# One block for the three stages of a deformable layer, smaller convolution rectangles, and a product moved to VectorE

## What is computed

```python
def deform_block(x, ow, ob, dw, pw, pb, K):
    offsets = conv2d(x, ow, ob, K // 2)             # 2*K*K channels: dy, dx for each tap
    out = deform_depthwise(x, offsets, dw, K, K // 2)  # bilinear samples of x at tap + offset, times dw[tap], summed over taps
    return conv2d(out, pw, pb, 0)
c3, c5, c7 = jnp.split(x, 3, axis=1)
out = jnp.concatenate([deform_block(c3, ..., 3), deform_block(c5, ..., 5), deform_block(c7, ..., 7)], axis=1)
return out * se_weight(out, fc1_w, fc2_w)           # gates from the mean and the maximum over the pixels
```

## Time and profile before

| | |
|---|---|
| median of the runs | 6606.05 us |
| the profiled execution, its own time | 6606.96 us |
| its span in the trace | 6604.7 us |
| PE busy | 88% of the span |
| VectorE busy | 73% |
| ACT busy | 59% |
| GpSimd busy | 12% |
| TensorE's granted clock, mean | 0.946 of full |

### The profile page before, as it was taken

How to read it: one execution, slowest core, us unless ns; L and a number is a source line. 1 busy time by engine, 2 the same in 40 slices (tenths; PEclk the granted TensorE clock), 3 DMA queues, 4 the chain that set the end, 5 groups by cost and what they waited for, 6 DMA issues and landing times. The chain is left out here.

```text
span 6604.7 us, 121718 instructions
## 1 busy us (share of the span) xinstructions
PE 5836.1 (88%) x45996; PEld 3998.1 (61%) x45996; DVE 4831.0 (73%) x10089; ACT 3905.2 (59%) x5362; POOL 782.4 (12%) x780
## 2 busy tenths in 40 slices
PE   5999999999977888988989989899889899699798
PEld 2554454454434556875568855588655688455598
DVE  6887887787765778887788877798777888344433
ACT  3766776676652557875567855578755787112142
POOL 2222211222202002001011000110100100000000
PEclk9999999999998999999989999999999899899898
DMA  4111111112104445545445545455544454211598
GB/s 145 43 56 55 40 44 55 49 39 59 44 23 134 105 105 123 124 110 118 105 117 118 119 97 129 99 126 121 117 105 108 114 124 111 96 46 41 145 234 199
DMA packets 198408, 651.46 MB, mean 99 GB/s; under 512 B 61753, under 2 KB 68849, under 8 KB 154915
## 3 DMA queue, kind: packets, MB, share of 16 engines
q1 hardware_dynamic: 177747, 604.65, 37.2%
q0 software_dynamic: 19968, 37.78, 2.2%
HBM read 538.56 MB, written 65.59 MB: 91 GB/s over the span
## 5 line engine op out<-in xcount | busy, mean ns | idle before, releaser
L2367 PE MATMUL b_p<-b_work,b_hkt 64*128 64x144 f32 (+37 forms) x27520 | 2116.5, 309 | 253.1 <-DVE b_acc L2238 149.7
L2367 PEld LDWEIGHTS b_p<-b_work,b_hkt 64*128 64x128 f32 x27520 | 1966.0, 195 | 479.9 <-DVE b_work L2313 283.2
L2313 DVE TENSOR_TENSOR b_work<-b_work 128x140 f32<-128x140 f32 (+26 forms) x5312 | 1605.5, 353 | 228.6 <-PE b_p L2367 174.7
L2208 ACT ACTIVATE b_work<-b_work,b_mcol 128x512 f32<-128x512 f32 (+6 forms) x1328 | 764.9, 647 | 1021.4 <-DVE b_work L2313 883.3
L530 ACT ACTIVATE a_ex<-a_p_t 128x1024 f32<-128x1024 f32 x512 | 523.9, 1023 | 427.3 <-PE a_p_t L466 424.5
L2212 ACT ACTIVATE b_work<-b_work,b_mrow 128x544 f32<-128x544 f32 (+6 forms) x1328 | 762.2, 645 | 0.0
L2238 DVE SCALAR_TENSOR_TENSOR b_acc<-b_p,b_dwc,b_acc 128x323 f32<-128x323 f32 (+14 forms) x1088 | 621.6, 574 | 184.5 <-PE b_p L2367 184.5
L596 DVE TENSOR_REDUCE a_nm<-a_p_x 128x1 f16<-128x1024 f32 x512 | 624.3, 1219 | 154.0 <-PE a_p_x L455 145.8
L1779 PE MATMUL b_p<-b_hp,b_ow 128*98 128x512 f32 x1568 | 721.4, 611 | 0.0
L602 DVE TENSOR_TENSOR a_el<-a_ex,a_eh 128x1024 f16<-128x1024 f32 x512 | 682.1, 1332 | 7.0 <-ACT a_eh L535 6.9
L535 ACT CAST a_eh<-a_ex 128x1024 f16<-128x1024 f32 x512 | 535.4, 1046 | 54.8 <-ACT a_ex L530 3.8
(11 more groups left out here) (224 smaller groups left out, 5811.6 us busy)
## 6 DMA issues: line engine op xcount, KB each, us to landing
b_work<-sampling_positions SPq DMA_DIRECT2D x666, 512.0 KB, 6.5
d_win<-merged_kernels SPq DMA_DIRECT2D x192, 263.0 KB, 6.7
b_xin<-x SPq DMA_DIRECT2D x24, 1024.0 KB, 9.8
a_xr<-in_x SPq DMA_DIRECT2D x12, 1536.0 KB, 10.2
x<-a_xr SPq DMA_DIRECT2D x9, 1536.0 KB, 6.1
b_xr<-x SPq DMA_DIRECT2D x13, 1024.0 KB, 18.2
x<-b_xr SPq DMA_DIRECT2D x13, 1024.0 KB, 4.6
a_xh<-in_x SPq DMA_DIRECT2D x8, 1536.0 KB, 8.6
```

The source lines that it names most:

```text
L2208: last = e.activation(rx[:, u, xo[c]:xo[c + 1]].rearrange("p (a b) -> p a b", a=H), pp[:, b, 1, :].rearrange("p (a b) -> p a b", a=H)[:, : ...
L2313: e.tensor_tensor(S[:, k % NS, 0:(r1 - r0) * w].rearrange("p (a b) -> p a b", b=w), rx[:, u, xo[cc]:xo[cc + 1]].rearrange("p (a b) -> p a ...
L2367: last = e.matmul(G[:, a0 - top:z0 - top, c0 - left:c1 - left], hkt[64 * s:64 * s + 64, SIDE * cr + cc, :], S[64 * s:64 * s + 64, k % NS, ...
```

## The change

1. **Stages of a pair in one block.** The body of a stage becomes a function `stage_of(pr, g)` that returns five stream functions. The layer is built in two versions. The one that runs first (`far=False`) has one block per pair, in which each engine runs its part of stages 0, 1 and 2 in turn. Where a block's end stood between two stages, waits on the earlier stage's semaphores stand now: SyncE waits for a slot of `pp`, ACT for `rx` and `ry` (their buffer numbers run on over the stages, `(tap + g) % 2`), PE for the last sum in `acc`.
2. **Far samples looked at once.** `decide` gathers all flags into one, `anyfar`. Behind the layer this is tested once. If it is set, the whole layer 1 is run again in the old form (`far=True`, a block per stage and `sample_far` behind each). Without it, that code is jumped over.
3. **Clearing of `acc`** for K = 3 and 5 moves from VectorE to GpSimd.
4. **Taps by rectangles.** The offset convolution begins with the inner tap, over all 512 columns. Every other tap covers only the pixels whose source lies inside the image, in rows and in columns.
5. **Head product on VectorE.** In layer 0 the product of line 570 moves from GpSimd's stream to VectorE's, into the same slot of the pipeline, behind the reciprocal. Its wait for `osum` is left out, since VectorE wrote it.

```diff
 (layer0, gpsimd: removed; vector: added)
+                    k = m - 5 - BEHIND
+                    if ends_head(k, end):
+                        hh = k // NT
+                        r = ROWS_OF[hh % 2]
+                        e.wait_ge(s_d4.sem, s_d4.at((b * HEADS + hh + 1) * 16))
...
+                        e.tensor_tensor(o[r:r + D, hh // 2 % PAIRS, :], osum[r:r + D, :, :]..., denb[r:r + D, :], ALU.mult).then_inc(s_n.sem, 1)
 (conv_matmul)
+def inner_first(K):
+    inner = K * K // 2
+    return [inner, *(tap for tap in range(K * K) if tap != inner)]
-            dy, dx = divmod(k, K)
+            dy, dx = divmod(inner_first(K)[k], K)
+            up, left = dy - K // 2, dx - K // 2
+            (a0, z0), (a1, z1) = (max(0, -up - 16 * n), min(16, H - up - 16 * n)), (max(0, -left), min(W, W - left))
-                e.matmul(bank_of(u[1])[0:M, :].rearrange("p (a b) -> p a b", b=W), ow[:, k * M:(k + 1) * M],
-                                hp[:, s, r0:r0 + 16, c0:c0 + W], start=(k == 0), stop=(k == K * K - 1))
+                e.matmul(bank_of(u[1])[0:M, :].rearrange("p (a b) -> p a b", b=W)[:, a0:z0, a1:z1], ow[:, (dy * K + dx) * M:(dy * K + dx + 1) * M],
+                                hp[:, s, r0 + a0:r0 + z0, c0 + a1:c0 + z1], start=(k == 0), stop=(k == K * K - 1))
 (decide)
+            if far:
+                e.tensor_scalar(wide[:, gj:gj + 1], fw[:], 0.0, None, ALU.is_gt)
+            e.scalar_tensor_tensor(sh["anyfar"][:], fw[:], 0.0, sh["anyfar"][:], ALU.is_gt, ALU.max).then_inc(s_fl.sem, 1)
 (stage_of: sync)
-                        for sem in taps[gp].all:
-                            e.sem_clear(sem.sem)
+                if g == 0:
+                    for sem in (*taps[1].all, *taps[2].all):
+                        e.sem_clear(sem.sem)
+                        elif g > 0:
+                            e.wait_ge(prev.s_ab.sem, prev.s_ab.at(2 * (last_in_slot(g - 1, b) + 1)))
                         read_positions(e, pp, g, tap, tp.s_pp[b])
...
                 read_positions(e, pp, nxt, 0, ahead)
-                e.wait_ge(ahead.sem, ahead.at(32))
+                if far or g == 2:
+                    e.wait_ge(ahead.sem, ahead.at(32))
 (gpsimd; removed from vector)
+                if K in QUARTERED:
+                    e.wait_ge(s_pw.sem, s_pw.at(stage * 4 + 4))
+                    e.memset(acc[:], 0.0).then_inc(tp.s_g.sem, 1)
 (scalar)
                     if tap >= 2:
                         e.wait_ge(tp.s_s.sem, tp.s_s.at(ITEMS1 * (tap - 1)))
+                    elif g > 0:
+                        e.wait_ge(prev.s_s.sem, prev.s_s.at(ITEMS1 * (LAST - 1 + tap)))
 (tensor)
+                if g > 0:
+                    e.wait_ge(prev.s_g.sem, prev.s_g.at(sums_of(g - 1)))
                 sums_in_taps(e, gp)
 (the loop, far=False)
+                with nc.Block() as block:
+                    @block.vector
+                    def _(e):
+                        for g in range(G3):
+                            stages[g][3](e)
 (program)
-        layer1(nc, sh, x1, t, x2)
+        layer1(nc, sh, x1, t, x2, False)
+        with nc.If(nc.values_load(sh["again"][0:1, 0:1], min_val=0, max_val=1) > 0):
+            layer1(nc, sh, x1, t, x2, True)
```

More of the change, by code:

```diff
@@ L1747, in layer1 @@
         s_cu = (s_cu0, s_cu1)
-        FL = 3
+        FL = 4
         SE = 5
@@ new lines, in layer1 @@
+        with nc.Fori(0, B // 2) as pr:
+            stages = [stage_of(pr, g) for g in range(G3)]
+            if far:
+                now, after = pr * 2, (pr + 1) % (B // 2) * 2
+                for g, K in enumerate(KS):
+                    nxt, (sync, gpsimd, scalar, vector, tensor) = (g + 1) % G3, stages[g]
+                    with nc.Block() as block:
+                        block.sync(sync)
+                        block.gpsimd(gpsimd)
+                        block.scalar(scalar)
+                        block.vector(vector)
+                        block.tensor(tensor)
+                    with nc.If(nc.values_load(wide[0:1, g:g + 1], min_val=0, max_val=1) > 0):
+                        sample_far(nc, sh, g, K, acc, ps, {"posd": posd[g], "minus": minus, "low": low, "Ed": t["b_E"], "hTd": hTd, "dw": t[f"b_dw{g}"], "x": xv, "b": now,
+                                                           "dcv": dcv, "dcvd": dcvd, "ow": ow, "owd": t["b_ow"], "xin": xin, "work": work}, tfar, s_far)
+                        with nc.Block() as block:
+                            @block.sync
+                            def _(e):
+                                read_positions(e, pp, nxt, 0, s_far["ld"])
+                                e.wait_ge(s_far["ld"].sem, s_far["ld"].at(32))
+                        clear(nc, [s_far["ld"].sem])
+            else:
+                with nc.Block() as block:
@@ L2221, in _ @@
+                        for g in range(G3):
+                            stages[g][2](e)
                     @block.vector
                     def _(e):
[L2223 to L2227 removed]
@@ L2379, in layer1 @@
-                with nc.If(nc.values_load(wide[0:1, g:g + 1], min_val=0, max_val=1) > 0):
-                    sample_far(nc, sh, g, K, acc, ps, {"posd": posd[g], "minus": minus, "low": low, "Ed": t["b_E"], "hTd": hTd, "dw": t[f"b_dw{g}"], "x": xv, "b": now,
-                                                       "dcv": dcv, "dcvd": dcvd, "ow": ow, "owd": t["b_ow"], "xin": xin, "work": work}, tfar, s_far)
-                    with nc.Block() as block:
-                        @block.sync
-                        def _(e):
-                            read_positions(e, pp, nxt, 0, s_far["ld"])
-                            e.wait_ge(s_far["ld"].sem, s_far["ld"].at(32))
-                    clear(nc, [s_far["ld"].sem])
+                        for g in range(G3):
+                            stages[g][4](e)
```

617 lines of the change are left out of this document (331 added, 286 removed).

## The result

The changed kernel takes **6382.1 us** (median of 4 runs, 6381.2 to 6391.0); the kernel before, beside it, 6604.9 us. The ratio is 0.9663, with an interval of 0.9646 to 0.968. The profiled execution's span went from 6604.7 to 6389.2 us, 215.5 us less.

What follows compares the result with a forecast made beforehand. PE was taken as the fullest engine in every window, with VectorE near it only in stage 2. The terms 61 + 8 + 24 + 62 + 8 + 3 + 2 = 168 us took 6607 to 6439, say 6440 us; range 6390 to 6500.

Steps and rivals of the forecast that it cites:

- the head product: Layer 0: 78 us more VectorE work against 60 us no longer held; together 2 us less, bounds -17 and +17.
- Boundaries inside a pair: Layer 1, stages 0 to 1 and 1 to 2: 4 x (6.5 + 8.7) = 61 us less, plus 8 us of clock.
- Between pairs: Layer 1: one of two jumps and the clearing ahead of S go; 3 x 7 + 2.6 = 24 us less.
- Rectangles: Layer 1's offset convolution: time follows columns; 62 us less for K = 7, 8 for stage 2, 3 ahead of the loop.
- The tail of layer 1: Last pair's stage 2: the single test of `again` replaces its test, one jump for one, 0 us.
- (a): PE stays the bound and the boundaries close: 6400 to 6475 us, chance 0.68.
- (d): Everything pays in full: rectangles 73 + 17 + 3, layer 0 17, clock twice 8 us; 6396 us, chance 0.06.
- (b): VectorE or ACT takes over where PE gets shorter: 6485 us, chance 0.16.
- (c): A stage's first positions land late, 5 us at eight boundaries, and less clock is won back: 6488 us, chance 0.06.
- (e): Float32 products writing rows of 29 to 31 run slower per record; with 0.1 us each 6733 us, chance 0.02.
- (f): One flag is set and layer 1 runs a second time: some 3600 us more, 10,000 us, chance 0.01.
- Clearing on GpSimd: Layer 1: first pair gains 2.6 us; by the collision rule alone, clearing `acc` would hold S 1.8 us eight times, 14 us.

Runs made afterwards that it cites:

- pool_two_in: The kernel after, with an extra two-input product on GpSimd for each head in layer 0, its result unread: 6423.0 us, 41 us more than the kernel after.
- joined_only: The kernel after with full rectangles and the head product back on GpSimd: 6506.6 us, ratio 0.9843 to the kernel before.
- blocks_kept: The kernel after, but each stage in a block of its own, with no test of a flag: 6411.2 us, 29 us more than the kernel after.
- rect_only: The kernel before, with only the offset convolution's rectangles of the kernel after: 6535.4 us, ratio 0.9894 to the kernel before.
- grid_dve: The kernel after, with 48 two-input grid additions in layer 1's loop moved from GpSimd to VectorE: 6400.4 us, 18 us more than the kernel after.
- pool_one_in: The kernel after, with an extra one-input product on GpSimd for each head in layer 0, its result unread: 6403.9 us, 22 us more.

## Why the prediction was wrong, point by point

**The step that failed** is the last of the terms, the head product: "VectorE does not gain 78 us of work but 78 - 60 = 17 ... Together -2", with bounds of -17 and +17. Measured alone it is a gain of 29 to 32 us, outside both bounds, and that is more than half of the miss. The rows were read rightly: line 602 is held for 60 us, all of it went away, and VectorE's busy time in the stretch rose by 17 us as forecast (the windows below). So were the 8 us at the projection: PE's wait for the product went from 16.7 to 8.9 us. The netting was wrong. A microsecond held and a microsecond of added work have different prices. By the table above, held time at 0.8 is worth 48 us and the projection 8, and 78 us of work at a quarter cost 20. That is 36 us gained as an estimate, where the stretch lost 34. The forecast had priced neither: it subtracted one from the other and took a third of the rest.

```profile
108.50:1973.00 1864.50, 1696.05 (x6718) 892.70 (x6717) 1480.28 (x1468) 1254.99 (x1448) 389.32 (x512) 0.97 0.17 47
```

```profile
107.50:1938.00 1830.50, 1682.71 (x6718) 890.75 (x6717) 1497.73 (x1532) 1254.28 (x1448) 220.42 (x448) 0.98 0.17 47
```

Of the 34 us PE's idle time has 21. Its waits for the other engines fell from 163.9 to 144.1 us in sum. The other 13 are PE's busy time, for the same 6718 records: the granted clock was 0.98 instead of 0.97. What each wait did to the clock is not shown. Why held time is dearer is argued from where the waits stand (that for line 602 went from 10.8 to 1.6 us, and is 22.4 in pool_two_in), not shown.

**Boundaries inside a pair: right.** 4 x (6.5 + 8.7) was forecast; the timelines give 7.5 and 9.3, since the copies and second transposes take 1.75 and 2.2 us and not 2.8 after the sums. The records of line 1921 are back at 3.60 us, as forecast. The mean clock rose from 0.946 to 0.955. With the two levels that is, as an estimate, 2 x 0.054 x 6605 = 713 us at the lower one before and 575 after, 138 us less. By the traces about half of these lay in PE's idle time, where nothing was to be done. **Between pairs: right.** The holes are 5.8 us on average (6.5 forecast), and sums to first item lost 7.7 us (7). joined_only puts the whole at 95 in its trace, against 93. That a taken branch out of the window already fetched makes an engine stall is what the Trainium skill says in "Runtime: NRT & Kernel Launch", section "Instruction fetch mechanics". The holes agree, and in blocks_kept a block's end without a jump leaves a smaller one, 2.2 us.

**Rectangles: right alone, perhaps short in company.** Time follows columns (9.3% busy for 10.4%). The forecast took 85% for K = 7 because VectorE would hold some back, and half for stage 2. In rect_only stages 0 and 1 gave 4 x (2.8 + 11.8) = 58 us against 62, stage 2 some 14 against 8. With the joined block it is 75 and 13: the full 73 for K = 7. That is the second part of the miss, up to 15 us, and it is no larger than the intervals.

**The tail of layer 1**, counted 0 as "one jump for one", gave 6 us in the kernel after, and 3 in joined_only. The jump stood in front of the last pointwise products and now stands behind the layer. By the two rows above the hole before them went from 6.42 to 1.93 us and the products from 6.56 to 3.97, together 7.1 us. VectorE's idle time before layer 2's first instruction rose from 10.3 to 14.2 us, so 3.9 of it were given back there. Layer 2's first transposes wait for a transfer in both, and start 5.8 us nearer to the loop's end.

**Rivals.** (a) took place in its mechanism, and its 6400 to 6475 was missed through the layer 0 term. (d) was nearest in time (6396). It had the rectangles in full, which the runs leave possible, and 17 us for layer 0, which gave 32; whether its larger clock term came can't be told, with joined_only at 95 us by its trace and 100 by the medians, against 93 and 101. (b) did not take over: PE's waits for sums grew by 12 us, and the loop still lost 175. (c) was there as a wait and not as a price: ACT waits for positions as this row of the kernel after says, but seven taps cover it on PE.

```profile
ACT b_near_work L2252 <- DMA b_near_work<-sampling_positions_near: 80.2, 6, 20.1
```

(e) is refuted by line 1791. (f) did not occur: no record of the second form of layer 1 is in the trace of the kernel after.

**Clearing on GpSimd.** In the trace of the kernel after, 27 records of line 2352 overlap a clearing, and they are 0.07 us longer in sum than the median of their form. The Trainium skill ("GPSIMD Engine Reference", section "Key points") says that GpSimd contends with VectorE instructions that have two SBUF inputs. Read as if any GpSimd work did so, as the prediction read it, that would have made 14 us, as an estimate; for clearing the trace does not agree with that reading.

## What to carry to other kernels

Do not subtract added work from held time one for one. In layer 0 of this kernel, a product that a neighbour engine stretched from 1.2 to 3.4 us cost 0.8 to 1.0 of the held time. Short added work on the same engine, with a fifth of its time free, cost a quarter of itself at first and a half as the engine filled. Price the two separately, by the product made tiny and by the product made twice. Do not carry the result over without a run either: the same move in layer 1 (grid_dve) cost 18 us, although VectorE had less to do. And a stage boundary is worth taking apart into the test with its jump and the block's end, since the first was half to two thirds of it here.

## What the runs showed of the hardware

How long a two-input VectorE product is held depends on the GpSimd operation beside it. In layer 0, 64 products of two inputs (133 us busy) held line 602 for 52 us, 0.39 us per us; 64 of one input (192 us) held it for 19 us, 0.10 per us. The single records show how. A pair from pool_one_in, and one from pool_two_in:

```profile
434.07 2.76 POOL L570 TENSOR_SCALAR a_spare<-a_wp 48x1024 f32<-48x1024 f32 x1 [23.42 <-DMA a_denb<-score_sums_inverse]
434.11 2.07 DVE L602 TENSOR_TENSOR a_el<-a_ex,a_eh 128x1024 f16<-128x1024 f32 x1
```

```profile
1002.76 1.89 POOL L570 TENSOR_TENSOR a_spare<-a_wp 48x1024 f32<-48x1024 f32 x1 [9.93 <-DMA a_denb<-score_sums_inverse]
1002.81 2.92 DVE L602 TENSOR_TENSOR a_el<-a_ex,a_eh 128x1024 f16<-128x1024 f32 x1
```

In pool_one_in, 25 records of line 602 begin 0.04 to 0.84 us after the start of a GpSimd product. All end 2.11 to 2.14 us after it, whenever they began. Their own time is 1.21 us, so they were held until 0.9 us, a third of the product's 2.8. Those that begin after 0.9 us take 1.21 us. In pool_two_in the 25 such records end 2.97 to 3.00 us after the start of a product of 1.9 us, held until 1.76 us, nearly its whole length.

In layer 1 of the kernel after, line 2352's excess over the median of its own form was 67.5 us beside 100.5 us of two-input operations, 18.3 us beside 185 us of one-input ones (line 1773, without casts and copies), and next to nothing beside clearings (0.07 us over 27 records). Clearing 128 x 2048 takes much the same on both engines, 1.80 us on GpSimd and 1.77 on VectorE.
